# A state-space and MLP kernel on one core: an accumulating DMA, an earlier statistics step, and two operands that change memory

## What is computed

```python
x_ssm, z = split(x @ w_in.T + b_in);  z = silu(z)
dt = softplus(x_ssm @ w_dt.T + b_dt);  Bm, Cm = x_ssm @ w_B.T + b_B, x_ssm @ w_C.T + b_C
for n in 16 states:                       # A = -exp(A_log)
    h[n] = scan over t: exp(A[:, n] * dt[t]) * h[n] + dt[t] * Bm[t, n] * x_ssm[t]
y = sum_n h[n] * Cm[:, n] + D * x_ssm
x3 = layernorm(x2 + (y * z) @ w_out.T + b_out) * gamma + beta
x4 = layernorm(x3 + layernorm(x3 + 0.5 * (silu(h(x3) @ w1 + b1) @ w2 + b2)))   # h: the MLP's own norm
```

## Time and profile before

| | us |
|---|---|
| median of 3 runs | 1091.46 (1090.75 to 1092.55) |
| the profiled execution, its own time | 1090.75 |
| its span, first to last instruction | 1089.0 |
| busy in the span: PE / DVE / ACT / POOL | 982.5 / 929.1 / 840.1 / 715.1 |

### The profile page before, as it was taken

The page is one execution under the profiler, slowest core; times in us unless marked ns, Lnnn a source line. Parts: engine busy times, 40 slices in busy tenths (PEclk is TensorE's granted clock), DMA queues, the critical chain, the costliest instruction groups (busy, mean ns, idle before and its releaser), DMA issues. The chain is left out here.

```text
span 1089.0 us, 17906 instructions
## 1 busy us (share of the span) xinstructions
PE 982.5 (90%) x5612; PEld 744.1 (68%) x5612; DVE 929.1 (85%) x1234; ACT 840.1 (77%) x1633; POOL 715.1 (66%) x603
## 2 busy tenths in 40 slices
PE   6999999999978999998668599999999999996987
PEld 4777777777754555555547487777778777775776
DVE  7999999999963897965799999999999999999751
ACT  7778878878746668767867889898898988886733
POOL 3456466766761111323789989998989998989530
PEclk9999999999998999999778799999999999999899
DMA  6444434433415002112998777487766758767301
GB/s 186 127 143 113 138 110 141 122 94 116 122 50 195 0 1 78 39 39 89 247 167 182 134 160 153 130 173 148 174 145 172 145 144 180 155 138 151 79 1 39
DMA packets 93921, 133.86 MB, mean 123 GB/s; under 512 B 8706, under 2 KB 48642, under 8 KB 93828
## 3 DMA queue, kind: packets, MB, share of 16 engines
q1 hardware_dynamic: 93828, 132.73, 49.7%
HBM read 116.45 MB, written 14.16 MB: 120 GB/s over the span
## 5 line engine op out<-in xcount | busy, mean ns | idle before, releaser
L2346 DVE TENSOR_TENSOR_SCAN ob<-bank_a,h,ob 128x512 f32<-128x512 f32 x128 | 160.2, 1269 | 15.3 <-POOL ob L2566 9.1
L2346 DVE TENSOR_TENSOR_SCAN oa<-bank_a,h,oa 128x512 f32<-128x512 f32 x128 | 159.7, 1268 | 13.4 <-ACT h L2032 9.8
L1491 POOL TENSOR_TENSOR oa<-ob,x1T 128x1024 f32<-128x1024 f32 x8 | 18.8, 2354 | 129.5 <-DVE ob L1391 129.5
L1828 PE MATMUL bank_m<-w,f_h 128*128 128x256 f32 x448 | 102.9, 379 | 0.0
L2023 ACT ACTIVATE bank_a<-s,A 128x512 f32<-128x512 f32 x128 | 86.8, 684 | 17.3 <-DVE ob L2346 9.8
L2023 ACT ACTIVATE bank_a<-dtc,A 128x512 f32<-128x512 f32 x128 | 86.9, 684 | 15.1 <-DVE oa L2346 7.9
L1768 PE MATMUL bank_y<-ident,ob 128*128 128x128 f32 x512 | 71.8, 286 | 24.2 <-DVE ob L2352 12.9
L1828 PEld LDWEIGHTS bank_m<-w,f_h 128*128 128x128 f32 x448 | 83.6, 190 | 13.8 <-issue 3.6
L1768 PEld LDWEIGHTS bank_y<-ident,ob 128*128 128x128 f32 x512 | 62.5, 148 | 36.1 <-DVE ob L2352 15.4
L883 POOL TENSOR_TENSOR xd<-xs,L 128x512 f32<-128x512 f32 x32 | 33.9, 1060 | 75.7 <-DVE xs L662 75.7
L1768 PE MATMUL bank_y<-ident,oa 128*128 128x128 f32 x512 | 73.2, 290 | 10.7 <-DVE oa L2352 10.6
(11 more groups left out here) (405 smaller groups left out, 2920.7 us busy)
## 6 DMA issues: line engine op xcount, KB each, us to landing
Bb<-CB_rows SPq DMA_DIRECT2D x128, 256.0 KB, 5.9
Cb<-CB_rows SPq DMA_DIRECT2D x128, 256.0 KB, 5.2
abc<-decays SPq DMA_DIRECT2D x32, 512.0 KB, 4.4
Ebc<-ramps SPq DMA_DIRECT2D x64, 128.0 KB, 3.0
uT<-in_uT SPq DMA_DIRECT2D x8, 512.0 KB, 4.5
u<-in_u SPq DMA_DIRECT2D x8, 512.0 KB, 3.9
x_tokens<-x2s SPq DMA_DIRECT2D x8, 512.0 KB, 3.0
x_rows<-x1T SPq DMA_DIRECT2D x8, 512.0 KB, 3.6
```

The source lines that it names most:

```text
L1828: i = e.matmul(to, f_h[:, k, c * CH:(c + 1) * CH], w2[:, k, :], start=False, stop=(c % 2 == 1 and k == KF - 1))
L2346: e.tensor_tensor_scan(s[:, k, :], p_a[k][:, :], s[:, k, :], h0[:, n, k:k + 1], ALU.mult, ALU.add).then_inc(v_s, 1)
```

## The change

Four edits, all in the last stage:

1. POOL's addition of beta to x2 (`shifted`) becomes a DMA that POOL issues and that adds beta's row, read from DRAM, to x2 in SBUF; `summed` waits for its landing. The half-size additions of the last block stay, and their semaphore count is adapted.
2. DVE does `stats4` right after scan(8,0); product(7) and scan(8,1) come behind it.
3. The factor of state 4's first half goes to `bank_c` in place of `bank_a[0]`. ACT makes it right after decay(3,1), ahead of both `silu_up`; it waits for product(1), and spread_C(3) waits for scan(4,0). decay(5,0) waits for scan(3,0).
4. The product of state 2 reads the row of C from its SBUF buffer; spread_C(2) is gone, and load_C(6), which reuses that buffer, waits for product(2).

```diff
+            beta_row = d["everywhere"].rearrange("(a o n) -> a o n", a=1, o=1)[:, :, sum(n for _, n in EVERYWHERE) - DM:]
...
                 def load_C(b, n):
...
+                        elif (n - 4) % NS == UNSPREAD:
+                            e.wait_ge(v_g, vector_made(NS * b + n - 3))
                         else:
-                            e.wait_ge(a_c, vector_made(NS * b + n - 3))
+                            e.wait_ge(a_c, spread(NS * b + n - 3))
...
                 def decay(b, n, k):
...
-                    after(e, v_s, 2 * (NS * b + n - 1) + k + 1)
-                    e.activation(p_a[k][:, :], dtc[b % 2][:, k, :], ACT.Exp, scale=A[:, k, n:n + 1]).then_inc(a_a, 1)
+                    if (n, k) == (4, 0):
+                        e.wait_ge(v_g, vector_made(NS * b + 2))
+                    elif (n, k) == (5, 0):
+                        e.wait_ge(v_s, 2 * (NS * b + 3) + 1)
+                    else:
+                        after(e, v_s, 2 * (NS * b + n - 1) + k + 1)
+                    e.activation(factor(n, k)[:, :], dtc[b % 2][:, k, :], ACT.Exp, scale=A[:, k, n:n + 1]).then_inc(a_a, 1)
...
                         decay(cur, 3, 1)
+                        decay(cur, 4, 0)
                     if 0 <= last < NB - 2:
                         silu_up(last, 0)
-                    if live(cur):
-                        spread_C(cur, 2)
-                    if 0 <= last < NB - 2:
                         silu_up(last, 1)
                     if live(cur):
                         silu_z(cur)
                     if live(cur):
-                        decay(cur, 4, 0)
+                        decay(cur, 4, 1)
                         carry(cur, 2)
                     if live(nxt):
                         evac_x(nxt, 0)
                     if live(cur):
-                        decay(cur, 4, 1)
                         spread_C(cur, 3)
...
-                    e.tensor_tensor(prod[n % 2][:, :, :], state[(NS * b + n) % 4][:, :, :], both(p_c[:, :]), ALU.mult).then_inc(v_g, 1)
+                    e.tensor_tensor(prod[n % 2][:, :, :], state[(NS * b + n) % 4][:, :, :], both((Cb[n] if n == UNSPREAD else p_c)[:, :]), ALU.mult).then_inc(v_g, 1)
...
                     if live(post):
                         scan(post, 8, 0)
-                        product(post, 7)
-                        scan(post, 8, 1)
                     if 0 <= last < NB - 1:
                         stats4(last, 0)
                         stats4(last, 1)
                     if live(post):
+                        product(post, 7)
+                        scan(post, 8, 1)
                         scan(post, 9, 0)
...
                 def shifted(b):
                     e.wait_ge(v_pre, 2 * b + 2)
-                    e.sem_inc(step, 1)
-                    e.tensor_tensor(x2, x2, rowwise(bet), ALU.add).then_inc(p_xb, 1)
+                    e.dma_start(x2, beta_row.to_broadcast([P, NC, DM]), accum_op=ALU.add).then_inc(ld_beta, DMAS)
...
                 def summed(b):
                     e.wait_ge(p_gam, b + 1)
-                    e.wait_ge(p_xb, b + 1)
+                    e.wait_ge(ld_beta, DMAS * (b + 1))
```

More of the change, by code:

```diff
@@ L1566, in build @@
             p_b, p_l3, p_xb, p_gam, p_add, p_l4, p_l6 = (d_sem("p_" + n) for n in ("b", "l3", "xb", "gam", "add", "l4", "l6"))
-            ld_xT, ld_x2, st_o = (d_sem(n) for n in ("ld_xT", "ld_x2", "st_o"))
+            ld_xT, ld_x2, st_o, ld_beta = (d_sem(n) for n in ("ld_xT", "ld_x2", "st_o", "ld_beta"))
             pair, single = (p_m[0], p_m[2]), p_m[1]
@@ L1573, in build @@
             half = slice(0, 2), slice(2, 4)
-            p_g, on_pool = d_sem("p_g"), (0, 12, 14)
+            p_g, on_pool, UNSPREAD = d_sem("p_g"), (0, 12, 14), 2
             def pool_made(count):
@@ L1580, in vector_made, with spread, factor @@
                 return count - pool_made(count)
+            def spread(count):
+                return vector_made(count) - count // NS - (1 if count % NS > UNSPREAD else 0)
+            def factor(n, k):
+                return p_c if (n, k) == (4, 0) else p_a[k]
             def made(e, count):
@@ L2021, in decay @@
                         e.wait_ge(a_sp, b + 1)
-                    after(e, v_s, 2 * (NS * b + n - 1) + k + 1)
-                    e.activation(p_a[k][:, :], dtc[b % 2][:, k, :], ACT.Exp, scale=A[:, k, n:n + 1]).then_inc(a_a, 1)
+                    if (n, k) == (4, 0):
[5 more added lines that the diff above has]
+                    e.activation(factor(n, k)[:, :], dtc[b % 2][:, k, :], ACT.Exp, scale=A[:, k, n:n + 1]).then_inc(a_a, 1)
                 def spread_C(b, n):
                     e.wait_ge(ld_C[n % 4], DMAS * (4 * b + n // 4 + 1))
-                    after(e, v_g, vector_made(NS * b + n))
+                    if n == 3:
+                        e.wait_ge(v_s, 2 * (NS * b + 4) + 1)
+                    else:
+                        after(e, v_g, vector_made(NS * b + n))
                     e.activation(p_c[:, :], Cb[n % 4][:, :], ACT.Copy).then_inc(a_c, 1)
@@ L2345, in scan @@
                     s = state[(NS * b + n) % 4]
-                    e.tensor_tensor_scan(s[:, k, :], p_a[k][:, :], s[:, k, :], h0[:, n, k:k + 1], ALU.mult, ALU.add).then_inc(v_s, 1)
+                    e.tensor_tensor_scan(s[:, k, :], factor(n, k)[:, :], s[:, k, :], h0[:, n, k:k + 1], ALU.mult, ALU.add).then_inc(v_s, 1)
                 def product(b, n):
                     e.wait_ge(v_s, 2 * (NS * b + n) + 2)
-                    e.wait_ge(a_c, vector_made(NS * b + n + 1))
+                    if n == UNSPREAD:
+                        e.wait_ge(ld_C[n % 4], DMAS * (4 * b + n // 4 + 1))
+                    else:
+                        e.wait_ge(a_c, spread(NS * b + n + 1))
                     after(e, pe_y, NS * b + n - 1)
-                    e.tensor_tensor(prod[n % 2][:, :, :], state[(NS * b + n) % 4][:, :, :], both(p_c[:, :]), ALU.mult).then_inc(v_g, 1)
+                    e.tensor_tensor(prod[n % 2][:, :, :], state[(NS * b + n) % 4][:, :, :], both((Cb[n] if n == UNSPREAD else p_c)[:, :]), ALU.mult).then_inc(v_g, 1)
                 def gate(b, p):
@@ L2415, in end_sum @@
                     e.wait_ge(v_m, 4 * p + 1)
-                    e.wait_ge(p_xb, Z + p + 1)
+                    e.wait_ge(p_xb, p + 1)
                     e.tensor_tensor(xl[Z % 2][:, half[p], :], xl[Z % 2][:, half[p], :], x2[:, half[p], :], ALU.add).then_inc(v_m, 1)
```

## The result

The changed kernel takes 1099.65 us (median of 4 runs, 1097.65 to 1101.54), the kernel before 1091.76 (4 runs): ratio 1.0056, 95% interval 1.0032 to 1.0079. On the prediction's base of 1091.46 the ratio makes 1097.6, inside the range (to 1098.5), but the forecast was 1092.0 and no change. The interval of the ratio reaches from 1095.0 to 1100.1 on that base, across the range's upper end, so that the range held is in part luck. It went the way of the slower rival, which had a chance of 0.21. The profiled execution took 1099.15 us, its span 1097.2.

A forecast was written before the change was run, and what follows sets the result against it. DVE, PE, POOL and ACT were all taken as busy within 10% of the block's length. Terms -0.5, +1.1, +0.7, +0.5 and -0.6 gave +1.2 us on 1090.75: 1092.0, no change; range 1086 to 1098.5.

The forecast's parts named there:

- slower rival: POOL's stretch from beta to summed: late sum holds DVE at stats4; 1 us in each block, 1099; chance 0.21.
- step on beta's DMA: POOL's beta addition (2.37 us) becomes a DMA issue; priced 0 in this block, 0.3 to 1.2 earlier where POOL was late.
- The added traffic: State 8's row of B beside the added 512 KB: slack of 1.2 us covers it; price 0, upper bound 4.7.
- The landing without the traffic: State 8's row of B, issued at 787.2 behind load_C(6), lands after the median 5.9 us, at 793.1.
- Statistics ahead: stats4 before product(7) on DVE: POOL's wait of 1.60 goes, DVE's 0.55 grows by 0.45, gate 0.15 to 0.2 earlier.
- my terms for late sums: Blocks where summed comes after DVE is ready for stats4: +1.1 in the first, +0.7 for two more, +0.5 in the last.
- SiLU region: State 4's factor and state 2's product: DVE's wait of 1.43 becomes a gain of 0.1 at scan(7,1); -0.1 us per block.
- The faster rival: The gain around ACT's Silu run survives because ACT has room from 791.8 to 801.3: 1.24 for five blocks, 1085; chance 0.25.
- SBUF operand: product(2) reads two SBUF inputs while POOL works: into(5) is over, so DVE waits for nothing; price 0, bounds 0 and 2.37.
- POOL's issue: POOL issuing the DMA for beta: taken as 1.4 us, bounds 0 and 4.7.
- late-landing rival: The accumulation into x2 lands later than 15 us after its issue: 3 us late in 7 blocks, +21, 1112; chance 0.05.
- A stopped issue: product(2) stops POOL's DMA issue until 786.7, norm36 is 0.1 to 0.4 late: 1.8 over the forecast, 1094; chance 0.08.

The follow-up runs named there:

- the earlier issue: The changed kernel with load_B(8) put ahead of load_C(6) in SP's list, so state 8's row of B is issued earlier: 1091.15 us, ratio 0.9983 to the kernel before.

## Why the range held and the forecast failed

The sign is that of the slower rival. The forecast failed in the step on beta's DMA, in one term: the price 0 for what the added 512 KB do to the row of state 8.

- **The added traffic.** I gave it 0, with 4.7 as the upper bound. With the full traffic from DRAM and the late issue, the row lands 8.1 to 10.3 us after its issue in six of the seven blocks (9.0 and 10.3 in the two long ones), and into(8) waits 1.4 to 3.8 us there. With the same late issue and a sixteenth of the traffic it lands 4.2 to 5.9 us after it, and into(8) does not wait. So the term is about 4 us on that landing, inside the bound and more than the slack.
- **The landing without the traffic: too long, if anything.** I took the median of the span, 5.9. In the kernel before, this row was slower, 7.7 in the block of the rows and 6.1 to 8.1 over the seven; issued late without added traffic it takes 4.4 to 5.2. A landing read at one place in the list does not hold for another. The slack of 1.2 was there: 1.8 in the block shown for edits 3 and 4 alone.
- **Late issue and traffic need each other** for the wait at into(8). The late issue alone gives none (1.0005 and 1.0007), the traffic with the early issue gives none (1.0035, 0.9999 and 0.9983, where single rows of state 9 are late instead). Three removals take the loss away: less traffic (0.9949), beta from SBUF (0.9931), the earlier issue (0.9983).
- **The slower rival's own account** was half right. Its source, into(8)'s row, is shown. Its transmission, stats4 ahead of product(7) turning lateness into DVE's wait, is not needed for the loss: with the statistics behind, the time is the same (1.0059). At most it takes back the 0.3% that the statistics bring alone. POOL's chain, into(8) to into(10) and on, is late either way. That its time, 1099, was near is luck: it added 1 us in each block, while DVE waits 2.2 for summed and part of that is made up elsewhere.

The other steps:

- **Statistics ahead: wrong in size.** The step held that the table load stands behind the wait for scan(8,1) and that the gate could come only 0.15 earlier. In the changed kernel's ACT the load starts as soon as the instruction before it has ended, 3.2 us before that scan ends:

```profile
810.60 1.28 ACT L2038 ACT_TABLE_LOAD   x1
813.82 0.69 ACT L2038 ACTIVATE bank_a<-dtc,A 128x512 f32<-128x512 f32 x1 [1.95 <-DVE oa L2361]
```

  With the 0.45 of added wait gone from the sum, a block gains 0.46 (63.44 against the 63.9 of the earlier trace rows). Moved alone the statistics are a gain of 0.3%, not a loss; my terms for late sums (+1.1, +0.7, +0.5) were a loss that this run does not show: its DVE waits for the sum 2.8 us in all.
- **SiLU region: right in size for an undisturbed block.** -0.1 was predicted; edits 3 and 4 added to the statistics took 0.18 from one. The wait of 1.43 moved on, but not quite as said: with beta from SBUF it is 0.54 before scan(4,1), 0.41 before product(4) and 0.51 before product(5), and none is left before scan(7,1), where I had kept 0.4. The faster rival's 1.0 did not appear, not even where product(2) became 1.1 us shorter (63.26 against 63.25). That ACT and what hangs on evac_x bound that stretch is my reading; the 0.51 is ended by PE. Over the whole kernel the two edits bring nothing alone (1.0005).
- **SBUF operand: right for the change, and for a reason that matters.** Product(2) took 1.20 to 1.22 in six of eight blocks, and 1.94 and 3.32 where a late POOL multiplication overlapped it. Without the DMA it takes 2.2 to 3.3 in seven blocks. In an undisturbed block that costs nothing (63.26), as said above. So the length of this product leans on the beta edit, which the prediction did not say; its cover was given as "into(5) is over", while the real one was that POOL's addition is gone.
- **POOL's issue: right.** 1.34 us measured, 1.4 estimated. Landing 10.4 (9.4 to 15.0), inside the 15 allowed; the late-landing rival did not occur.
- **A stopped issue: refuted.** In the next block of the changed kernel POOL reads

```profile
853.89 1.34 POOL L2595 DMA_DIRECT2D s<-in_everywhere  x1
855.30 0.60 POOL L2599 TENSOR_SCALAR ve<-st 128x8 f32<-128x8 f32 x1
```

  beside product(2) at 854.64, which held from there to 855.85. In six of the seven blocks product(2) overlaps the issue, in the block from 785 us it even began first (789.24 against 790.04), and the six issues take 1.34 to 1.36; the one without a product beside it took 1.50. The small POOL instruction after the issue, 0.20 where no such product runs, is stretched to the product's end. The Trainium skill ("SBUF — State Buffer", SBUF: two separate sides) says that a DMA from GpSimd is starved while DVE holds the shared ports in one of its two-port modes, and, as inferred there, that a `tensor_tensor` takes the read interface only, which descriptor writing does not need. For this product the trace agrees with the second sentence; I had used only the first.

What stays open: why edits 2 to 4 with POOL's addition (1.0007) are 0.8% behind the same with beta from SBUF, when undisturbed blocks are equal (63.26 and 63.25). The profiled executions differ by 3.2 us over the seven blocks, the medians by more. DVE's wait for summed is 5.8 us against 2.0, which fits a sum that comes earlier by about 1 us, but no run isolates it. Nor was it tried whether the DRAM source is slow because 128 partitions read the same 1 KB four times, or for another reason.

## What to carry to other kernels

Before traffic is added beside a transfer that was moved later, ask for the landing under that traffic and compare it with the time of the consumer; here a slack of 1 to 2 us in most blocks did not survive half a megabyte that made the landing 4 us longer, while either edit without the other left the row in time. A constant that a DMA adds or broadcasts may be better read from an SBUF copy that is already there than from DRAM: here that one argument turned 1.0056 into 0.9931. Edits that look independent can cover each other, here an SBUF operand whose product keeps its 1.2 us only because another edit took POOL's addition away, so time them in combination before one is dropped.

## What the runs showed of the hardware

- An accumulating DMA of 512 KB into SBUF, issued by POOL, occupies POOL 1.34 us (0.93 for 32 KB, 1.26 for 256 KB) and lands, from DRAM, in 10.3 to 12.2 us (medians of five kernels) for 512 KB, 6.5 for 256 KB and 3.5 for 32 KB; from SBUF 512 KB take 7.3 and 7.8 (two kernels).
- Its packets take 3.1 to 3.4% of the 16 DMA engines' span from DRAM and 2.1 to 2.3% from SBUF, at the same count and bytes. The median landing of the rows of B is 5.7 to 6.2 us in the kernels without it, 6.7 to 7.9 beside the one and 6.5 beside the other.
- A DVE product with two SBUF inputs (1.2 us) takes 1.7 to 3.3 us in the three kernels in which POOL adds beta (2.4 us) around it; beside POOL's issue of a DMA both keep their length (1.21 and 1.34 us in the block shown).
- An ACT_TABLE_LOAD (1.28 us) runs before the wait of the ACTIVATE for which it is made: in the changed kernel at 810.60, with the wait ending at 813.8.
